# Destination rows by one-hot products in the attention logits, signed planes for the second tensor product on GpSimd, and one load for four block words in the attention sums

## The reference

```python
s_n, v_n = _equiv_layernorm(s, v, gamma_s, beta_s, gamma_v)
msg_s = (s_n @ Ws_src)[src] + (s_n @ Ws_dst)[dst]
msg_v = jnp.einsum('ncx,cd->ndx', v_n, Wv_src)[src] + jnp.einsum('ncx,cd->ndx', v_n, Wv_dst)[dst]
y0, y1 = (rsh[:, 0], rsh[:, 1:4])
w1 = rbf @ W_rbf
m1_s, m1_v = _cg_tp(msg_s, msg_v, y0, y1, w1[:, :CS], w1[:, CS:2 * CS], ...)
a = (m1_s @ W_alpha).reshape(e, H, AS_)
a = jnp.sum(jnp.where(a > 0, a, 0.2 * a) * alpha_dot, axis=-1, keepdims=True)
...  # softmax of a over the edges of a destination: alpha
val_s = m1_s @ Ws_val
val_v = jnp.einsum('ecx,cd->edx', m1_v, Wv_val) * jax.nn.sigmoid(val_s @ Wg)[..., None]
m2_s, m2_v = _cg_tp(jax.nn.sigmoid(val_s), val_v, y0, y1, w2_ss, w2_sv, w2_vs, w2_vv0, w2_vv1)
hs = (m2_s @ Ws_vlin).reshape(e, H, AS_)
hv = jnp.einsum('ecx,cd->edx', m2_v, Wv_vlin).reshape(e, H, AV, 3)
agg = jax.ops.segment_sum(alpha * concat(hs, hv), dst, num_segments=n)
```

## Time and profile before

| | |
|---|---|
| median of 3 executions | 6518.27 us (6517.92 to 6519.3) |
| the profiled execution | 6522.98 us, its span 6521.2, granted clock 0.885 |
| DVE, PE, POOL, ACT busy | 75%, 74%, 65%, 32% of the span |
| logits stage | about 1259 to 3705 us |
| in it, 1600 to 3600 us | DVE 1798.0, PE 1694.5, POOL 1408.2, ACT 1336.3 us of 2000 |

### The profile page before, as it was taken

How to read it: one execution, slowest core, us unless ns; L and a number is a source line. 1 busy time by engine, 2 the same in 40 slices (tenths; PEclk the granted TensorE clock), 3 DMA queues, 4 the chain that set the end, 5 groups by cost and what they waited for, 6 DMA issues and landing times. The chain is left out here.

```text
span 6521.2 us, 160966 instructions
## 1 busy us (share of the span) xinstructions
PE 4857.5 (74%) x45499; PEld 3781.0 (58%) x45500; DVE 4858.6 (75%) x11101; ACT 2086.6 (32%) x6090; POOL 4225.5 (65%) x4249
## 2 busy tenths in 40 slices
PE   5666667388888888888888667776676677777775
PEld 3444445277777777777777556644444464444444
DVE  5777775589888988889888754567777756666665
ACT  1001002166666666666666400211000111001001
POOL 5777774177777777777777245267777727777771
PEclk8888888699999999999999899988888887777777
DMA  3333332133333333333333166222222212222221
GB/s 108 92 92 91 93 91 62 47 91 94 91 92 91 89 92 91 92 90 90 91 92 91 43 170 184 69 73 72 72 72 72 73 39 70 69 69 69 69 69 36
DMA packets 401393, 545.13 MB, mean 84 GB/s; under 512 B 144934, under 2 KB 283318, under 8 KB 401180
## 3 DMA queue, kind: packets, MB, share of 16 engines
q0 software_dynamic: 193920, 331.22, 20.9%
q1 hardware_dynamic: 207388, 212.84, 11.6%
HBM read 464.79 MB, written 78.90 MB: 83 GB/s over the span
## 5 line engine op out<-in xcount | busy, mean ns | idle before, releaser
L797 POOL DMA_INDIRECT e_rows<-tab,e_idx x2424 | 2291.1, 945 | 813.9 <-issue 697.4
L1066 POOL DMA_INDIRECT acc<-tabx,a_idx x1616 | 1686.2, 1043 | 871.7 <-issue 468.0
L842 PE MATMUL e_wps<-e_w,e_hidT 64*128 64x192 f32 (+1 forms) x4848 | 792.4, 461 | 876.8 <-DVE e_hidT L913 874.1
L842 PEld LDWEIGHTS e_wps<-e_w,e_hidT 64*128 64x128 f32 x4848 | 539.6, 250 | 1080.9 <-DVE e_hidT L913 967.8
L827 PE MATMUL e_win<-e_feat,e_ohy 128*32 128x96 f32 (+1 forms) x19392 | 1027.7, 330 | 22.1 <-DVE e_feat L907 19.5
L827 PEld LDWEIGHTS e_win<-e_feat,e_ohy 128*32 128x32 f32 x19392 | 707.3, 131 | 452.2 <-issue 301.2
L898 DVE TENSOR_TENSOR e_feat<-e_wps,e_rows 128x256 f32<-128x256 f32 x606 | 257.5, 425 | 833.3 <-DMA e_rows<-tab,e_idx 763.3
L907 DVE TENSOR_TENSOR e_feat<-e_wps,e_rows 128x384 f32<-128x384 f32 (+1 forms) x1616 | 720.4, 498 | 0.0
L1129 PE MATMUL a_c<-acc,a_buffer 128*128 128x64 f32 (+1 forms) x4848 | 625.4, 272 | 121.6 <-ACT a_buffer L1107 121.6
L1129 PEld LDWEIGHTS a_c<-acc,a_buffer 128*128 128x128 f32 (+1 forms) x4848 | 590.9, 192 | 143.7 <-issue 143.7
L816 ACT ACTIVATE e_idx<-src 128x4 int32 (+1 forms) x606 | 123.3, 204 | 1598.5 <-DMA e_rows<-tab,e_idx 1576.4
(11 more groups left out here) (251 smaller groups left out, 7828.0 us busy)
## 6 DMA issues: line engine op xcount, KB each, us to landing
h_d<-a_buffer SPq DMA_DIRECT2D x202, 322.0 KB
s_hin<-h_d SPq DMA_DIRECT2D x202, 322.0 KB, 3.1
e_rows<-tab,e_idx POOLq DMA_INDIRECT x2424
e_ein<-in_e64T SPq DMA_DIRECT2D x202, 128.0 KB
acc<-tabx,a_idx POOLq DMA_INDIRECT x1616
a_ein<-in_e_h SPq DMA_DIRECT2D x202, 64.0 KB
e_ein<-in_e16T SPq DMA_DIRECT2D x202, 32.0 KB
tab<-p_rows SPq DMA_DIRECT2D x36, 160.0 KB
```

Source lines behind the costliest of these rows:

```text
L797: pool.indirect_dma_start(out=rows[:, s, t, :], out_offset=None, in_=k.tab0, in_offset=bass.IndirectOffsetOnAxis(ap=idx[:, s, t:t + 1], ax ...
L842: mm = pe.matmul(wps[:, e, 2 * u + j, 0:WC], hidT[half, edges], w2[half, :], start=True, stop=True)
L1066: pool.indirect_dma_start(out=rows[:, b, q, :], out_offset=None, in_=table, in_offset=bass.IndirectOffsetOnAxis(ap=idx[:, b, end, q:q + 1] ...
```

## The change

- **Destination rows.** The destination gathers go. SP loads 128 rows in a row of `tabx1`, from the group's first destination on (`near`; a register read from `k.ctl` gives the row), and the group's 512 destinations, broadcast to all partitions (`ends`). DVE compares them with the partition's node number (`pick`, a one-hot of 128 x 512). PE forms, for each tile, the one-hot times `near` plus the identity times `msg`, once for the 64 scalar columns and once for the 96 vector columns (`both_ends`, 16 products a group), into PSUM banks shared with the radial weights (`a_rad`), and DVE's `head` reads them there; its add of the ends is gone. `tabx1` has 128 rows more, and layer 0's projection fills them from a cleared buffer before its own stores. A group that spans 32 destinations or more (a count of extra blocks over zero in `k.ctl`) sets `k.mixed`, and `attention_general` then repeats the logits with gathers.
- **Signs.** One harmonic is stored negated (POOL flips it), so that dot and cross are one subtract of two sets of planes and one add. In the first product DVE does both (512 and 128 elements in place of a reduce and two subtracts). In the second DVE makes the nine planes, and POOL does two subtracts and an add into `z` (`comb_ops`).
- **Monopole.** The y0 of the first product is multiplied into the radial input by POOL (`mono`), and ACT copies the weights in one operation for four.
- **Order on PE.** The second map runs ahead of all turns; its third block writes the scalars' bank. The new products stand between the turns.
- **Sums.** DVE loads four block words with one instruction every fourth group, and waits for its last add without the increment behind it. The iota for the one-hots stands in PSUM.

Cut to its core:

```diff
...
+                if L == 0:
+                    sp.wait_ge(cleared, 1)
+                    sp.dma_start(k.tabx1[k.NP:k.NP + P, :], k.acc_all[:, 0:XD]).then_inc(padded, 16)
+                    sp.wait_ge(padded, 16)
...
+def unpacked_blocks(eng, k, word, more):
+
+    eng.reg_alu(more, word, 8, ALU.logical_shift_right)
+    eng.reg_alu(word, word, 255, ALU.bitwise_and)
+    return (eng.snap(word, min_val=0, max_val=k.NBLK - 2),
+            eng.snap(more, min_val=0, max_val=k.NBLK))
...
-                    for rows, table, end, signal in ((msg, k.tabx0, 0, src_in), (far, k.tabx1, 1, dst_in)):
-                        for q in range(TPG):
-                            pool.indirect_dma_start(
-                                out=rows[:, b, q, :], out_offset=None, in_=table,
-                                in_offset=bass.IndirectOffsetOnAxis(ap=idx[:, b, end, q:q + 1], axis=0),
-                            ).then_inc(signal[b], 16)
...
-                    v.wait_ge(src_in[b], uses(s, i, 0) * (16 * TPG) + 16 * TPG)
-                    hold(v, k, dst_in[b], uses(s, i, 0) * (16 * TPG) + 16 * TPG)
-                    v.tensor_tensor(m, m, far[:, b, :, :], ALU.add).then_inc(head_ops, 1)
...
-                    v.tensor_reduce(red[:, :, :], vy[:, :, 0, :, :].rearrange("p t x c -> p t c x"), AX.X, ALU.add).then_inc(head_ops, 1)
...
-                    cross(cr, vy, head_ops)
...
-                    v.tensor_reduce(zz[:, :, S:96], ty[:, :, 0, :, :].rearrange("p t x c -> p t c x"), AX.X, ALU.add).then_inc(mid_ops, 1)
-                    cross(pair[:, :, :, V:2 * V], ty, mid_ops)
...
+                sp.dma_start(mono[:, b, :],
+                             a["y0_h"][bass.ds(g + 4, 1), :, :].rearrange("o k e -> k (o e)")).then_inc(ein_in[b], 16)
+                if not scattered:
+                    if not isinstance(g, int) or g >= 0:
+                        hold(sp, k, pick_ready, g + 1)
+                    sp.dma_start(ends[:, b, :], a["dst_rows"][bass.ds(g + 4, 1), :].to_broadcast([P, GE])).then_inc(ends_in[b], 16)
+                    sp.load([reg], k.ctl[0:1, bass.ds(g + 4, 1), 0:1])
+                    first = sp.snap(reg, min_val=0, max_val=k.NP)
+                    sp.dma_start(near[:, b, :], k.tabx1[bass.ds(first, P), :]).then_inc(dst_in[b], 16)
...
+                for q in range(TPG):
+                    pool.indirect_dma_start(
+                        out=msg[:, b, q, :], out_offset=None, in_=k.tabx0,
+                        in_offset=bass.IndirectOffsetOnAxis(ap=idx[:, b, 0, q:q + 1], axis=0),
+                    ).then_inc(src_in[b], 16)
...
+                hold(pool, k, ein_in[b], i * 32 + 64)
+                pool.tensor_tensor(ein[:, b, :], ein[:, b, :], mono[:, b, :], ALU.mult).then_inc(ein_ready, 1)
...
+                pool.tensor_tensor(ybuf[:, b, :, 4], ybuf[:, b, :, 4], minus[:, :], ALU.mult).then_inc(y_ready, 1)
...
+                pool.tensor_tensor(zz[:, :, 2 * V:8 * V].rearrange("p t (u w) -> p t u w", w=3 * V)[:, :, :, 0:V],
+                                   planes[:, :, 0:2, :], planes[:, :, 4:6, :], ALU.subtract).then_inc(comb_ops, 1)
+                pool.tensor_tensor(zz[:, :, 7 * V:11 * V].rearrange("p t (u w) -> p t u w", w=2 * V)[:, :, :, 0:V],
+                                   planes[:, :, 2:4, :], planes[:, :, 6:8, :], ALU.subtract).then_inc(comb_ops, 1)
+                hold(pool, k, comb_ops, g * 3 + 1)
+                dot = zz[:, :, 2 * V:3 * V]
+                pool.tensor_tensor(dot, dot, planes[:, :, 8, :], ALU.add).then_inc(comb_ops, 1)
...
+                act.activation(wy[:, :, :].rearrange("p (b t) c -> p b t c", b=2), wps[:, :, :, 0:192], ACT.Copy).then_inc(wy_ready, 1)
...
+        def both_ends(b, q, o, vectors):
+            out, cols = (mv[:, q, :], slice(S, XD)) if vectors else (ms[q // 2][:, q % 2, :], slice(0, S))
+            if scattered:
+                pe.matmul(out, k.ident[:, :], far[:, b, q, cols], start=True, stop=False)
+            else:
+                pe.matmul(out, pick[:, o, q * P:(q + 1) * P], near[:, b, cols], start=True, stop=False)
+            return pe.matmul(out, k.ident[:, :], msg[:, b, q, cols], start=False, stop=True)
...
+                for q in range(TPG):
+                    product(q, c2[:, q, 0:64], P, "L1_c4", zT, 1)
+                    product(q, c2[:, q, 64:128], P, "L1_c5", zT, 2)
+                hold(pe, k, sig_ready, g + 1 if inside(g, n) else n)
+                for q in range(TPG):
+                    mm = product(q, scal[:, q, 164:228], 96, "L1_c3", zT, 0)
+                mm.then_inc(c2_ready, 1)
...
+            turn_feat(0)
+            if ahead:
+                if isinstance(g, int) and g == -2:
+                    pe.wait_ge(wready, 1)
+                hold(pe, k, ein_ready, g + 3)
+                for j in range(2):
+                    for u in range(2):
+                        rows = slice(NB * u, NB * u + NB)
+                        pe.matmul(wps[:, u, j, :], ein[rows, b, j * P:(j + 1) * P], wr[rows, :], start=True, stop=True)
+                hold(pe, k, src_in[b], uses(s, i, 2) * (16 * TPG) + 16 * TPG)
+                hold(pe, k, dst_in[b], uses(s, i, 2) * ends_step + ends_step)
+                if not scattered:
+                    hold(pe, k, pick_ready, g + 3)
+                both_ends(b, 0, o, False)
+                both_ends(b, 1, o, False).then_inc(w_ready, 1)
+            turn_feat(1)
+            if ahead:
+                both_ends(b, 0, o, True)
+                both_ends(b, 1, o, True)
+                both_ends(b, 2, o, False)
+            turn_feat(2)
+            if ahead:
+                both_ends(b, 2, o, True)
+                both_ends(b, 3, o, True)
+                both_ends(b, 3, o, False).then_inc(m_ready, 1)
+            if inside(g + 1, n):
+                hold(pe, k, f_taken, (g + 2) * 3)
+                if not isinstance(g, int) or g >= 0:
+                    hold(pe, k, mid_ops, g * MID + 3)
...
+            v.tensor_scalar(pick[:, s % 2, :], ends[:, b, :], k.node[:, bass.ds(g, 1)], None, ALU.is_equal).then_inc(pick_ready, 1)
...
+            for j in range(2):
+                v.tensor_tensor(feat[:, 2 * j:2 * j + 2, 0:192].rearrange("p t (o c) -> p t o c", o=2)[:, :, :, 0:S],
+                                wy[:, 2 * j:2 * j + 2, 0:2 * S].rearrange("p t (o c) -> p t o c", o=2),
+                                over(ms[j], 2, 2), ALU.mult).then_inc(head_ops, 1)
+            with_planes(vy, mv, y).then_inc(head_ops, 1)
+            v.tensor_tensor(pair[:, :, :, 0:V], over(wy[:, :, 2 * S:160], 2, 3), m, ALU.mult).then_inc(head_ops, 1)
+            hold(v, k, head_ops, at + 3)
+            flat = vy.rearrange("p t j x c -> p t (j x c)")
+            v.tensor_tensor(dc.rearrange("p t j c -> p t (j c)"), flat[:, :, 0:4 * V], flat[:, :, 4 * V:8 * V], ALU.subtract).then_inc(head_ops, 1)
+            hold(v, k, head_ops, at + 5)
+            v.tensor_tensor(dc[:, :, 0, :], dc[:, :, 0, :], flat[:, :, 8 * V:9 * V], ALU.add).then_inc(head_ops, 1)
+            v.tensor_tensor(pair[:, :, :, V:2 * V], over(wy[:, :, 160:192], 2, 3), dc[:, :, 1:4, :], ALU.mult).then_inc(head_ops, 1)
+            hold(v, k, head_ops, at + 6)
+            v.tensor_tensor(feat[:, :, S:96].rearrange("p (b t) c -> p b t c", b=2), wps[:, :, :, 192:224],
+                            dc[:, :, 0, :].rearrange("p (b t) c -> p b t c", b=2), ALU.mult).then_inc(head_ops, 1)
+
...
                 def ones_at(first, half):
                     tiles = 2 * TPG
-                    v.tensor_tensor(oh[:, half, :, :, :].rearrange("p u t n -> p (u t) n"), over(k.iota[:, :], 1, tiles),
+                    v.tensor_tensor(oh[:, half, :, :, :].rearrange("p u t n -> p (u t) n"), over(iota, 1, tiles),
                                     over(k.key_all[:, bass.ds(first * TPG, tiles)], 2, NB), ALU.is_equal).then_inc(oh_ready, 1)
+                v.tensor_copy(iota, k.iota[:, :]).then_inc(iota_ready, 1)
+                v.wait_ge(iota_ready, 1)
                 ones_at(0, 0)
                 ones_at(2, 1)
                 v.memset(k.acc_all[:, 0:half], 0.0).then_inc(cleared, 1)
                 cur = v.alloc_register("s_block")
-                regs = registers(v, "s_dve")
+                words = [v.alloc_register(f"s_dve_word{u}") for u in range(U)]
+                more_reg = v.alloc_register("s_dve_more")
                 def link(ins):
                     ins.then_inc(more_link, 1)
                 def step(g, s, i):
                     if inside(g, n):
                         o, j = s, g
-                        block_, more = packed_blocks(v, k, j, regs)
+                        if s == 0:
+                            v.load(words, k.ctl[0:1, bass.ds(g, U), 4])
+                        block_, more = unpacked_blocks(v, k, words[s], more_reg)
                         if isinstance(g, int) and g == 0:
                             v.wait_ge(cleared, 2)
                         hold(v, k, win_ready, g + 1)
```

(13 more changed lines are left out.)

658 lines of the change are left out of this document (350 added, 308 removed).

## The result

The changed kernel takes 7228.11 us (7168.7 to 7295.38, 4 runs) against 6518.51 (6517.92 to 6519.3, 4 runs): a ratio of 1.106, with a 95% interval of 1.098 to 1.114. The ratio leaves out the slowest of the four, whose granted clock was 0.856 where the others had 0.863 to 0.874. The direction was forecast, the size was not: the forecast was 6960 with a range to 7130. Its executions also spread over 1.8%, where those of before agree within 0.02%.

The account below looks back on a forecast made before the run. PE's own step, with its handshakes, was taken to bound the logits stage, with DVE as long. +450 (PE's products), -15 (sums) and +7 (rest) on 6522.98 gave 6965, set at 6960 us; range 6750 to 7130.

Parts of the forecast that it names:

- What bounds the stage: Logits stage: PE's handshakes with ACT set 11.85 us a group; DVE is as long, so relieving one alone buys nothing.
- A product's price: PE, logits stage: 16 added products are 32 records at 0.107 us, 3.42 us; group 14.1 us, +450 us in all.
- The clock: PE, logits stage: granted clock of 1.00 (2.4 GHz) taken from before; a clock under 1.00 "would void the sum".
- The rival at 7200 us: Logits stage: no gap is filled, or POOL's three operations come late; group 15.3 us, +690 us; chance 0.09.
- the first rival: Logits stage: PE absorbs the new products in free holes, DVE sets 9.9 us a group, -394, 6116 us; chance 0.09.
- GpSimd and the transfers: Logits stage: POOL's 7.4 to 10.7 us a group stays hidden under 14.1; DMA share stays 0.35; no cost.
- Sums: Sums stage: one four-word load replaces four on DVE, 0.1 us a group, -15 us (-25 to 0).
- The rest: Outside those stages: first projection's stores begin near 46.5 us, DVE 5 us late, setup and semaphores 2; +7 us.

Follow-up runs that it names:

- no_add: The kernel before with VectorE's add of the two ends over 4 elements a partition instead of 640: 6520.85 us, ratio 0.9998.
- two_banks: The kernel before with PE's turns alternating between two PSUM banks, which also changes the second map's order: 6603.14 us, ratio 1.014.
- order3: The kernel before with PE's products in the changed kernel's order and 16 identity-by-identity products where the new ones stand: 7489.15 us, ratio 1.147.
- one_product: The changed kernel without the identity product of each pair, 8 products a group less: 6986.78 us, ratio 1.072 to the kernel before.
- one_wait: The changed kernel with PE waiting for ACT's copy behind the second turn, ahead of six new products: 7500.68 us, ratio 1.150 to the kernel before.
- order_of_after: The kernel before with the changed kernel's PE order, run in a session of lower granted clock; ratios of this kernel there 1.085 and 1.084.

## Why the prediction was wrong

- **What bounds the stage**: right. PE sets the step, and DVE's relief alone is worth nothing (no_add). PE's relief alone was worth 0.3 us a group at the full clock, and less than nothing with the clock (two_banks).
- **A product's price**: right in mechanism, a little small. The 32 new records took 3.53 us (2619.71 to 2620.54, 2620.99 to 2622.27, 2622.72 to about 2624.14), 3.42 were taken; the three turns 1.36 for 1.22; the map 2.62 for 2.56; the gaps 0.70 for 0.57 (0.18 ahead of the radial products; 0.28 ahead of the new ones, where nothing was taken; 0.24 ahead of the first map, where 0.40 was, so that two errors nearly cancel); from the first map on 5.64 for 5.64. Together 14.53 for 14.09, +88 us. By the figure of the Trainium skill ("TensorE: Matmul & The Clock Gate", "Back-to-back issue gap"), about 81 ns a pair of load and matmul with 128 moving columns, an estimate for the 32 records is 2.6 us. The trace disagrees, at 0.110 each in fp32 with 64 and 96 moving columns, and decides.
- **The clock**: here the prediction failed. It carried the 1.00 of the earlier trace rows over to a queue with another order, named a lower clock only as what "would void the sum", and gave it no chance, no price and no part of the range. The runs showed 0.91 in its place, with 50 falls that cost some 225 us. Without them the time would be some 7228 - 225 = 7003 us, inside the range; this is an estimate. Nothing in the rows of before said that it would happen, so it belonged among the rivals. That the order and load of PE bring the falls is shown (order3); which piece of the order, and by what mechanism, stays open. The rival at 7200 us came near by its number but by luck and not by its mechanism: it has every group at 15.3, and 147 of 201 took 14.4 to 14.6.
- **A count in the first rival**: the group has 44 products, 88 records, and the turns' 24 make the 112. The text counts the turns twice; by its 0.107 a record the 112 take 12.0 us, so the rival stays unlikely.
- **GpSimd and the transfers**: right as far as the trace tells. POOL's three operations are not waited for by PE; no gap stands ahead of z's first turn.
- **Sums**: -41 us for -15. The term was priced by the loads' durations, 0.4 us in four groups, and not by the distance from add to add, which fell by 0.9.
- **The rest**: +9 for +7. The table's stores began at 46.15 us, where 46.5 was taken.

## What to carry to other kernels

Before work is moved onto an engine, find its own step: the loads of one iteration with each gap's cause. If its gaps are handshakes and its step equals the period, relief of a busier-looking engine is worth nothing, and each product added past the gaps costs its full price.

A granted clock of 1.00 was read from one queue of PE and holds for that queue. Here it was lost with another order of the same work, and with fewer rows in the same order; more work in the old order kept it. Give its loss a chance and a price whenever PE's order or its products change, and time such a change in several executions and on more than one chip.

Where an engine's queue is on the path, price a register load by the distances between the operations on both sides of it, and over a whole round: the pair that gains most is not the mean.

## What the hardware showed unasked

- The clock did not follow PE's busy share. It stayed at 1.00 with 1820 us busy in 2000 (the sixteen products in the old order) and fell with 1726 (one product for each pair).
- Its falls have a fixed place in the group: 2.1 to 2.9 us behind the start of a second map in the changed kernel, `one_product` and `order3`, and in `one_wait` also behind the idle stretch that it adds.
- Sixteen products of 32 rows a group took it to 0.65; the same with 128 rows left it at 1.00.
- In some sessions the kernel before took 9560 or 9326 us, one of them on a chip that had run it at 6521 earlier, with a granted clock of 0.68 to 0.69 over the program. DVE's busy time did not grow (4891 us for `order_of_after`, with the work of the kernel before's 4859). The ratio of the changed order in the kernel before was 1.085 there and 1.147 elsewhere.
